# Six small pads that move the tiles of a fused attention and mixture-of-experts kernel in SBUF

## The reference

```python
x = x + _layernorm(attn(_layernorm(x), Wq, Wk, fc1_w, fc1_b, fc2_w, fc2_b))
x = x + _layernorm(ffn(_layernorm(x), gate_w, gate_b, w1, b1, w2, b2))

# attn: one head; q and k are 1024 x 256 per sequence, rotated
exp_qk = where(causal, exp(q @ k.T / 16), 0)
o = exp_qk.sum(axis=-1)                  # one number per row
o = relu(o @ fc1_w.T + fc1_b) @ fc2_w.T + fc2_b

# ffn: 8 experts, each row goes to its best two
logits = flat @ gate_w + gate_b
h = gelu(flat @ W1e + b1e)               # 256 -> 1024
out = h @ W2e + b2e                      # 1024 -> 256, weighted, summed over two experts
```

## Time and profile before

| | |
|---|---|
| median of 3 runs | 705.41 us (705.11 to 705.66) |
| the profiled execution: its own time | 705.67 us |
| its span, first to last instruction | 703.9 us |
| TensorE matmul busy in the span | 563.0 us, 80% |
| VectorE busy | 484.4 us, 69% |
| ScalarE busy | 298.3 us, 42% |
| mean granted TensorE clock, as a share of 2.4 GHz | 0.898 |

### The profile page before, as it was taken

How to read it: one execution, slowest core, us unless ns; L and a number is a source line. 1 busy time by engine, 2 the same in 40 slices (tenths; PEclk the granted TensorE clock), 3 DMA queues, 4 the chain that set the end, 5 groups by cost and what they waited for, 6 DMA issues and landing times. The chain is left out here.

```text
span 703.9 us, 14366 instructions
## 1 busy us (share of the span) xinstructions
PE 563.0 (80%) x4174; PEld 508.2 (72%) x4175; DVE 484.4 (69%) x1571; ACT 298.3 (42%) x673; POOL 182.5 (26%) x153
## 2 busy tenths in 40 slices
PE   2768788684230899999999999999999999999700
PEld 1536373542110899999999999999899999999600
DVE  4988888686450676976666666669766666796547
ACT  3564657564210546533333333358242424653250
POOL 2000170624424231223232323232231313131300
PEclk9958879797565899999999999999999999999955
DMA  9970020211125535632232223246432323433286
GB/s 289 310 269 0 13 102 8 83 38 53 68 70 151 188 46 152 166 44 51 39 51 39 51 39 52 38 115 163 95 45 45 45 45 45 149 55 49 46 274 211
DMA packets 52876, 66.79 MB, mean 95 GB/s; under 512 B 4870, under 2 KB 47340, under 8 KB 52716
## 3 DMA queue, kind: packets, MB, share of 16 engines
q1 hardware_dynamic: 37740, 46.81, 20.9%
q0 software_dynamic: 14016, 18.56, 15.6%
q10 hardware_dynamic: 1088, 1.07, 0.5%
HBM read 38.26 MB, written 28.74 MB: 95 GB/s over the span
## 5 line engine op out<-in xcount | busy, mean ns | idle before, releaser
L1073 ACT ACTIVATE h<-pL,b_now 128x256 f32<-128x256 f32 x288 | 121.0, 471 | 244.7 <-PE pL L1139 243.8
L1052 POOL DMA_INDIRECT sum_y<-y,dest x72 | 115.5, 1605 | 319.7 <-DVE y L1204 308.7
L1139 PE MATMUL pL<-xeT_hi,w_lo 128*128 128x256 f32 x576 | 163.5, 284 | 6.0 <-issue 3.7
L1151 PE MATMUL pY<-w_hi,h_lo 128*128 128x256 f32 x576 | 164.2, 285 | 0.9 <-DVE h_lo L1177 0.7
L1139 PE MATMUL pL<-xeT_hi,w_hi 128*128 128x256 f32 x576 | 162.5, 282 | 0.0
L1139 PE MATMUL pL<-xeT_lo,w_hi 128*128 128x256 f32 x576 | 162.4, 282 | 0.0
L1151 PE MATMUL pY<-w_hi,h_hi 128*128 128x256 f32 x576 | 161.1, 280 | 0.0
L1151 PE MATMUL pY<-w_lo,h_hi 128*128 128x256 f32 x576 | 160.8, 279 | 0.0
L1139 PEld LDWEIGHTS pL<-xeT_hi,w_lo 128*128 128x128 f32 x576 | 109.3, 190 | 7.9 <-issue 4.6
L1151 PEld LDWEIGHTS pY<-w_hi,h_lo 128*128 128x128 f32 x576 | 108.5, 188 | 1.3 <-DVE h_lo L1177 1.3
L1139 PEld LDWEIGHTS pL<-xeT_hi,w_hi 128*128 128x128 f32 x576 | 109.3, 190 | 0.0
(11 more groups left out here) (185 smaller groups left out, 699.1 us busy)
## 6 DMA issues: line engine op xcount, KB each, us to landing
w_stage<-w SPq DMA_DIRECT2D x16, 1024.0 KB, 7.9
xt<-sorted_x SPq DMA_DIRECT2D x38, 260.0 KB, 2.7
sum_y<-fill SPq DMA_DIRECT2D x1, 4352.0 KB, 24.7
w_stage<-sum_y SPq DMA_DIRECT2D x8, 512.0 KB, 5.2
out<-z SPq DMA_DIRECT2D x8, 512.0 KB, 3.0
x_all<-x SPq DMA_DIRECT2D x3, 1024.0 KB, 8.7
sum_y<-y,dest POOLq DMA_INDIRECT x72, 3.8
sorted_x<-fill ACTq DMA_DIRECT2D x4, 260.0 KB, 5.6
```

The source lines that it names most:

```text
L1052: pool.indirect_dma_start(out=sum_y, out_offset=bass.IndirectOffsetOnAxis(ap=dest[:, i:i + 1], axis=0), in_=y[:, i, :], in_offset=None, co ...
L1073: a = act.activation(h[:, c, :], pL[:, bk, i * TM:(i + 1) * TM], ACT.Gelu, bias=b1_now[par][:, c:c + 1])
L1139: mm = pe.matmul(pL[:, bk, i * TM:(i + 1) * TM], w[:, 0, col], x[:, k, :], start=(k == 0 and w is lo), stop=(k == KC - 1 and x is xeT_lo))
L1151: mm = pe.matmul(pY[:, i, 0:D], s[:, c, rows], w[:, 1, c * D:(c + 1) * D], start=(c == 0 and s is h_lo), stop=(c == FC - 1 and w is lo))
```

## The change

Six tiles that nothing reads or writes are allocated between the others. No instruction is added, removed or moved: the order of every engine before and after is the same, row for row. Only addresses differ.

```diff
+        sb("pad_to_64", [P, 8], F32)
         w_stage = [sb(f"w_stage{i}", [P, 2, FC * D], F32) for i in range(2)]
...
+            sa("pad_consts", [P, 8], F32)
             wqk_hi = sa("wqk_hi", [P, KC, 2, D], F32R)
...
+            sa("pad_rows", [P, 8], F32)
             xn = sa("xn", [P, TB, D], F32)
...
+            sa("pad_hidden", [P, 8], F32)
             hidT = sa("hidT", [P, TB // 2, P], F32R)
...
+            sa("pad_x3", [P, 8], F32)
             x3T = sa("x3T", [P, KC, L], F32)
...
+            se("pad_to_128", [P, 24], F32)
             w_hi[1] = se("w_hi1", [P, 2, FC * D], F32R)
```

## The result

The changed kernel takes 696.03 us (median of 6 runs, 694.22 to 698.49) where the kernel before takes 705.26 (6 runs, 703.76 to 707.39): a ratio of 0.9878, 95% interval 0.9861 to 0.9895. It is 1.2% faster; 713.0 was forecast, 1.1% slower. The profiled execution took 695.66 us.

A forecast was written before the change was run, and what follows sets the result against it. PE's matmul pitch was taken to bound the expert stage. Expert tiles +7.1 us and projections +0.5, added to the profiled 705.67, gave 713.3, or 713.0 as median; own range 710 to 715 (chance 0.60), overall 694 to 715.

The forecast's parts named there:

- After it all 36 tiles have the alignment of expert 7's: Expert stage: the even experts' 32 tiles would slow to expert 7's 119.8 and 120.0 ns, 0.22 us a tile.
- the sum's +7.1 us: Expert stage: 32 even tiles at 0.22 us more each, all on the path because PE waits for nobody there.
- The first rival: Even expert tiles: operands aligned but 64 bytes apart avoid meeting in memory; 682 us, or 694; faster cases together 0.26.
- a picture of slices sweeping past each other: Expert matmuls: both operands' slices pass every 64-byte place, so 64 bytes more or less should not keep reads apart.
- Down to 110 ns, 682 us: First rival's full effect in the 32 even tiles, bounded by the transposes' 110 ns: -23 us.
- My half effect, 694: First rival with half the even tiles' excess gone: 694 us, as likely as the whole effect.
- "Everything at 0", pitch 240 and +0.5 us: Attention projections: all operands aligned, pitch from 233.3 to 240 ns, 1.3 us for four, mostly covered by VectorE; +0.5 taken.
- 13.3 x 2: Projections: expert 7's excess per 256 columns doubled for 512 columns, 26.6 ns, giving the pitch of 240.
- the 10.0 ns that the projections share with the second expert block: Projections' excess per 256 columns equals the even experts' second block's; used as evidence that the 32-byte offset matters.
- the no-change rival: Expert tiles: a coarser address property separates odd from even, so 64-byte alignment doesn't matter; 705.4 us, chance 0.14.
- Misaligned reads cost: Rows at 32 mod 64 touch an extra 64-byte piece; alignment saves up to 21 us, 684; counted within faster's 0.26.

The follow-up runs named there:

- all_zero: The changed kernel with 64 bytes less in the last pad, so every expert tile has both operands at the same place mod 256: 710.77 us, ratio 1.0094.
- The grid: Not a kernel variant: blocks of 96 f32r matmuls alone, over pairs of starts; d is moving start minus stationary start, mod 256; 113.3 to 120.0 ns steady.
- the parts run: Matmuls alone, without the reference's work, varying column counts, type and alternating starts; 512 columns take 226.7 ns at d = 0, 233.3 at 96 and 128.
- The fine run: Matmuls alone, stationary tile at 0, moving one at 0 to 240 in steps of 16 bytes, four entries each: 113.3 to 120.0 ns.
- mixed: proj_b with xeT at 240 mod 256, making the first expert block's distance 112 (xn also 128 bytes further): ratio 0.9913 to the kernel before.
- proj_b: The changed kernel with odd experts' operands also 64 mod 128 apart and xT moved 128 bytes, projections at d = 0: ratio 0.9861 to the kernel before.

## Why the prediction was wrong

**What held.** That nothing but the pitch sets the experts' time, that all of the change's effect would be in the even experts' tiles, expert 7 staying at 119.8 and 120.0, no effect on bf16 (216 ns before and after), gate (430) and DMA (`w_stage` 7.9 and 8.1 us): the profile after bears these out. The comparison I took my number from was measured rightly too. All tiles at the odd experts' pitch does cost what was forecast: all_zero is 0.94% slower, 1.1% was the forecast.

**The step that failed** is "After it all 36 tiles have the alignment of expert 7's", and with it the sentence that 64 bytes more or less should not keep two reads apart. I took the last six bits of each address as the property that the odd tiles' 120 ns comes from. The odd tiles had two properties, every operand at 0 mod 64 and both at the same place mod 256, and the trace of before couldn't separate them. The grid does: with both at 32 past a multiple of 64 it is 119.9 as well. The change gave the even tiles the first property and not the second. The address table showed that (weights at 0, `xeT` and `h` at 64 mod 128). So the sum's +7.1 us for them came as -9.0: 113.4 and 113.7 ns where 119.8 and 120.0 stood in it. The first rival named the combination, with two reads that meet as the cause. That the pitch hangs on the two starts together is shown; how the memory makes it so is not. I argued the rival down to a part of 0.26 with a picture of slices sweeping past each other. In that picture all distances that are multiples of 64 are alike; the grid has 120.0 at 0, 113.3 or 117.8 at 64 and 118.6 at 128.

**The size of the rival.** Down to 110 ns, 682 us, had its bound from transposes of 128 columns. No f32r block of 256 columns in any run is under 113.3, which puts the experts' part at 32 x 0.37 = 11.8 us, and 15 blocks at the second level take 3.1 of it. My half effect, 694, was near the 696.03 for another reason than I gave.

**The projections.** "Everything at 0", pitch 240 and +0.5 us for it, was wrong twice. By the table `wqk` went to 128 mod 256 and `xT` to 0, so d went from 96 to 128; the parts run has 233.3 for both, and 232.4 is what came. And at d = 0 they would have been fastest, 226.7: doubling the 256-column excess (13.3 x 2) was not allowed, since the two lengths order the distances differently. For the same reason the 10.0 ns that the projections share with the second expert block were a coincidence and no ground against the no-change rival: the one has d = 96, the other 32, and 256 columns at d = 96 take 120.0.

**The other rivals.** Misaligned reads cost: no, at the same distance a stationary operand at 32 past a multiple of 64 pays in the grid what one at 0 pays, 120.0 at d = 0 and 118.3 at 224. No change: no, and the 16-byte lines that the Trainium skill gives in SBUF — State Buffer, Specifications (TRN2), would by themselves make all these placements equal. The fine run finds 113.3 to 120.0 among multiples of 16. That loading weights steals nothing from the running matmul (the Trainium skill, TensorE: Matmul & The Clock Gate, Step-by-step: what each phase is for) doesn't fit the f32r rows: with the moving tile at 0 the stationary one's start alone takes the pitch from 113.3 to 120.0 ns. bf16, at the one placement tried, shows 109.2 and nothing to win.

## What to carry to other kernels

Where back-to-back f32r matmuls bound a kernel, compare the starts of the stationary and the moving tile with each other, mod 256, and measure a few distances of the kernel's own shapes alone before placing tiles: here 64 or 192 served 256 columns, 0 served 512, and distances of 0 and 96 were the worst for 256. When two groups of rows differ, list every property in which they differ, and ask which of them the change really gives; a rival that names a combination no row shows deserves a chance that fits that ignorance. And test a placement in the kernel: the distance that was best alone lost there, where the pair of starts was one that had not been measured.

## What the runs showed of the hardware

- The f32r pitch of 256 columns with 128 stationary ones, at a granted clock of 1.00, goes from 113.3 to 120.0 ns by the two operands' starts (and, at some distances, the entry), 5.9%, on three chips alike.
- At a distance of 64 or 192 there are two stable levels, 113.3 and 117.8 ns, and a stream of identical matmuls stays on either for a whole block; 32 (116.7 or 117.8) and 160 (117.4 or 118.7) have two as well. In mixed 32 of 36 second blocks sit on the worse level, with proj_b's same placement and another block ahead 5 do.
- The lowest pitch found is 17/16 of one column a cycle at 2.4 GHz, at 256 columns (113.3) and at 512 (226.7). What the seventeenth part is, no run shows.
- 128 moving columns take 111.7 ns at both distances tried, hardly less than 256 columns at their lowest; what bounds them no run separates.
